# A fused embedding, attention and expert kernel: a hardware loop written out, first loads on two semaphores, one fill in place of two, and a broadcast that reads SBUF instead of DRAM

## What is computed

```
h   = concat(x @ W_tok + pe,  text embedding of x_txt)            # (16, 1101, 128)
y   = layernorm(h)
q, k, v = y @ wq, y @ wk, y @ wv                                   # per head, 64 wide
o   = softmax(q @ k.T / 8) @ v
h   = h + concat_heads(o) @ head_kernel
f   = layernorm(h) * ln_scale + ln_bias
out = h + swiglu(f @ shared_in.T) @ shared_out.T + b
        + sum over the 2 best of 4 experts of the better group: weight_e * (swiglu(f @ expert_in.T) @ W_e.T + b_e)
```

## Time and profile before

| | us |
|---|---|
| three runs | 4684.33, 4683.44, 4683.88 |
| median | 4683.88 |
| the profiled execution's own time | 4684.45 |
| its span, first to last instruction | 4682.7 |
| TensorE busy | 4476.3 |
| VectorE, ScalarE, GpSimd busy | 3215.6, 2298.7, 2943.6 |

### The profile page before, as it was taken

The page is one execution under the profiler, slowest core; times in us unless marked ns, Lnnn a source line. Parts: engine busy times, 40 slices in busy tenths (PEclk is TensorE's granted clock), DMA queues, the critical chain, the costliest instruction groups (busy, mean ns, idle before and its releaser), DMA issues.

```text
span 4682.7 us, 93178 instructions
## 1 busy us (share of the span) xinstructions
PE 4476.3 (96%) x26597; PEld 3324.5 (71%) x26597; DVE 3215.6 (69%) x7726; ACT 2298.7 (49%) x5640; POOL 2943.6 (63%) x1803
## 2 busy tenths in 40 slices
PE   5999999999999999999999999999999999999996
PEld 3667767777677776767777677776767777677765
DVE  5557767677675776768677675776767677686754
ACT  1555545445544555545545444555445455455441
POOL 0776666666666666666666666666666666666661
PEclk7999999999999999999999999999999999999998
DMA  2111111111101111111111111111011111111000
GB/s 53 35 34 41 33 30 40 39 25 34 45 24 39 32 32 40 30 33 40 33 32 34 32 37 39 25 34 45 25 38 35 30 39 34 30 40 37 21 21 19
DMA packets 157061, 159.01 MB, mean 34 GB/s; under 512 B 66576, under 2 KB 148359, under 8 KB 156551
## 3 DMA queue, kind: packets, MB, share of 16 engines
q1 hardware_dynamic: 156551, 152.68, 13.4%
HBM read 59.63 MB, written 19.65 MB: 17 GB/s over the span
## 4 chain that ended last, share of the span: by engine, by line
PE 84%; issue 4%; DVE 4%; DMA 3%; ACT 3%; POOL 1%; DVEq 0%; ACTq 0%; SPq 0%; POOLq 0%
PE o_ps L791 23%; PE work L688 12%; PE scores L772 12%; PE scores L774 11%; PE work L747 9%; PE work L680 4%; PE work L731 3%; PE work L673 2%; DMA sums<-inverse_rows 2%; PE work L708 2%; PE work L699 2%; PE work L736 1%; ACT probs L877 1%; DVE part_max L935 1%; POOL sums L1165 1%
## 5 line engine op out<-in xcount | busy, mean ns | idle before, releaser
L1165 POOL TENSOR_TENSOR sums<-sums,probs 128x736 f32<-128x736 f32 (+3 forms) x1344 | 2363.4, 1758 | 838.7 <-ACT probs L877 780.8
L877 ACT ACTIVATE probs<-scores 128x368 f32<-128x368 f32 (+3 forms) x3456 | 1460.2, 475 | 1542.5 <-PE scores L774 1487.1
L935 DVE TENSOR_REDUCE part_max<-work 128x1 f32<-128x368 f32 (+3 forms) x3456 | 1655.3, 530 | 449.5 <-PE work L688 439.1
L772 PE MATMUL scores<-q_a,k_a 128*128 128x368 f32 (+3 forms) x3456 | 1191.7, 345 | 84.0 <-issue 43.3
L791 PE MATMUL o_ps<-probs,values 128*64 128x368 f32 (+1 forms) x6912 | 1219.2, 489 | 1.6 <-ACT probs L877 0.2
L774 PE MATMUL scores<-q_b,k_b 128*128 128x368 f32 (+3 forms) x3456 | 1147.5, 332 | 0.0
L688 PE MATMUL work<-k_a,q_a 128*128 128x368 f32 (+3 forms) x3456 | 928.8, 352 | 9.1 <-DMA q_a<-q_b 8.1
L791 PEld LDWEIGHTS o_ps<-probs,values 128*64 128x64 f32 (+1 forms) x6912 | 453.0, 138 | 539.0 <-issue 447.1
L772 PEld LDWEIGHTS scores<-q_a,k_a 128*128 128x128 f32 (+1 forms) x3456 | 636.3, 184 | 200.4 <-ACT probs L877 77.9
L688 PEld LDWEIGHTS work<-k_a,q_a 128*128 128x128 f32 (+1 forms) x3456 | 595.0, 185 | 234.2 <-issue 208.8
L774 PEld LDWEIGHTS scores<-q_b,k_b 128*128 128x128 f32 (+1 forms) x3456 | 639.9, 185 | 17.4 <-issue 4.2
(11 more groups left out here) (183 smaller groups left out, 4493.1 us busy)
## 6 DMA issues: line engine op xcount, KB each, us to landing
sums<-inverse_rows SPq DMA_DIRECT2D x192, 184.0 KB
k_a<-k_a SPq DMA_DIRECT2D x128, 184.0 KB, 2.7
q_a<-q_b SPq DMA_DIRECT2D x128, 184.0 KB, 2.7
k_a<-k_a SPq DMA_DIRECT2D x64, 183.0 KB, 2.7
q_a<-q_b SPq DMA_DIRECT2D x64, 183.0 KB, 2.7
resid_rows<-heads_t SPq DMA_DIRECT2D x16, 576.0 KB, 6.2
h_out<-resid_rows SPq DMA_DIRECT2D x16, 576.0 KB, 8.0
heads_t<-in_pe_table_dram SPq DMA_DIRECT2D x16, 512.0 KB
```

What stands on the lines that cost most here:

```text
L772: nc.tensor.matmul(o, k_a[p % 2][i][:, t * P:t * P + n], q_a[p % 2][i][:, c0:c0 + cw], start=True, stop=False)
L877: nc.scalar.activation(probs[0:n, slot(s), i, 0:cw], scores[0:n, h % SB, 0:cw], ACT.Exp, scale=DH ** -0.5).then_inc(probs_ready, 1)
L935: nc.vector.tensor_reduce(part_max[0:n, i * IMG + j if j < IMG else 2 * IMG + i, c:c + 1], w[0:n, 0:keys], AX.X, ALU.max).then_inc(drained ...
L1165: nc.gpsimd.tensor_tensor(acc, acc, probs[0:n, slot(s), :, 0:cw], ALU.add).then_inc(sums_done, 1)
```

## The change

Four edits are made together.

1. The middle batches are written out: `for b in range(1, B - 1)` in place of the hardware loop. All counts become constants.
2. The first loads are split over two semaphores. The six small ones (position, nesting and segment tables, text weights, gates) go on `small_loaded`; the 22 others stay on `raw_loaded`. TensorE's first wait is for the six; it waits for the 22 ahead of the weight transposes. The load of `wo` (256 KB) moves to the end of the loads.
3. Rows 64 to 127 of each `k_b` tile are filled with ones in one instruction. Rows 65 to 127 meet zeros of `q_b`, so products are unchanged.
4. The inverses are stored to `sums[0:2, q % 2, 1, :]`, two rows of SBUF, instead of DRAM, and spread from there.

```diff
+    small_loaded = sem("small_loaded")
...
-            sp.dma_start(pos_raw[:], pos[0:TXT, :]).then_inc(raw_loaded, 16)
+            sp.dma_start(pos_raw[:], pos[0:TXT, :]).then_inc(small_loaded, 16)
...
-            sp.dma_start(wo[:], head_w.rearrange("(a p) n -> p a n", p=P)).then_inc(raw_loaded, 16)
...
+            sp.dma_start(wo[:], head_w.rearrange("(a p) n -> p a n", p=P)).then_inc(raw_loaded, 16)
             sp.wait_ge(s_taken, 11)
...
-            pe.wait_ge(raw_loaded, 16 * 28)
+            pe.wait_ge(small_loaded, 16 * 6)
             pe.wait_ge(s_pool, 2)
...
+            pe.wait_ge(raw_loaded, 16 * 22)
             for g, group in enumerate(groups):
...
-        with eng.Fori(1, B - 1) as b:
+        for b in range(1, B - 1):
             iteration(loop, b - 1, b)
...
-                then(nc.vector.memset(k_b[r][i][64:128, :].bitcast(F32), 0.0))
-                nc.vector.memset(k_b[r][i][64:65, :].bitcast(F32), 1.0)
+                nc.vector.memset(k_b[r][i][64:128, :].bitcast(F32), 1.0)
...
-            sp.dma_start(inv_dram[q % 2].rearrange("(a n) -> a n", n=RW), inv_cols[:]).then_inc(cols_stored, 16)
+            two_rows = sums[0:2, q % 2, 1, :]
+            sp.dma_start(two_rows.rearrange("p (a n) -> p a n", n=RW), inv_cols[:]).then_inc(cols_stored, 16)
...
-            two_rows = inv_dram[q % 2].rearrange("(i n) -> i n", i=2)
+            two_rows = sums[0:2, q % 2, 1, :]
             sp.dma_start(sums[:, q % 2, 0, :], two_rows.unsqueeze(1).broadcast_to((2, DH, CHUNK))).then_inc(
                 inverse_loaded[q % 2], 16)
```

More of the change, by code:

```diff
@@ L229, in fusion_kernel @@
     text_dram = nc.dram_tensor("text_rows", (B, TXT, D), F32, kind="Internal").ap()
-    inv_dram = nc.dram_tensor("inverse_rows", (2, 2 * CHUNK), F32, kind="Internal").ap()
     resid_dram = nc.dram_tensor("resid_rows", (B, P, NT * D), F32, kind="Internal").ap()
@@ L318, in _ @@
             sp.dma_start(tok_i[:], x_txt).then_inc(loaded, 16)
-            sp.dma_start(pos_raw[:], pos[0:TXT, :]).then_inc(raw_loaded, 16)
[L320 to L324, removed]
+            sp.dma_start(pos_raw[:], pos[0:TXT, :]).then_inc(small_loaded, 16)
+            sp.dma_start(tab_raw[0:NEST, :], nest).then_inc(small_loaded, 16)
+            sp.dma_start(tab_raw[NEST:NEST + SEG, :], seg).then_inc(small_loaded, 16)
+            sp.dma_start(txt_wr[:], txt_w.rearrange("(a p) n -> p a n", p=P)).then_inc(small_loaded, 16)
+            sp.dma_start(gates_raw[0:2, :], group_w).then_inc(small_loaded, 16)
+            sp.dma_start(gates_raw[2:2 + E, :], expert_w).then_inc(small_loaded, 16)
             sp.dma_start(in_raw[:, 0], sh_in.rearrange("(a p) n -> p a n", p=P)).then_inc(raw_loaded, 16)
@@ L344, in _ @@
             sp.wait_ge(s_stored, 16)
-            sp.wait_ge(raw_loaded, 16 * 28)
+            sp.wait_ge(raw_loaded, 16 * 22)
         in_turns = [(in_raw[:, w, a, :], P) for w in range(2) for a in range(4)]
@@ L390, in _ @@
         def _(act):
-            act.wait_ge(raw_loaded, 16 * 28)
+            act.wait_ge(raw_loaded, 16 * 22)
             v = attn_raw[:].rearrange("p (h w) n -> p w h n", w=3)
```

## The result

The changed kernel takes 4842.17 us (median of four, 4837.42 to 4842.66) against 4683.66 us. The ratio is 1.0336, 95% interval [1.0318, 1.0354]: slower by 158 us, where the prediction said 59, in a range that ended at 4795. The profiled execution has a span of 4840.0 us; the one of before had 4682.7, so the traces differ by 157.3 us and can be set against each other.

A forecast was written before the change was run, and what follows sets the result against it. TensorE, busy 96% of the span, plus its waits was taken as the bound. From 4684.45 us, -11.8 - 5.5 - 22.5 + 34.5 + 1.7 + 34.5 + 25.5 + 2.3 = +58.7 gave 4743 us, range 4630 to 4795.

The forecast's parts named there:

- The start: Before the first scores: small loads on their own semaphore, -11.8 us, and one fill for two, -5.5 us.
- The loop inside a batch: Inside a middle batch, straight code was to cost TensorE the same as the loop: 0 us.
- The sign of being wrong that I had named: Straight middle batches taking over 97.3 us from one L699 to the fifth after it, a fetching cost put at nothing.
- The loop at the boundaries: Last score tile to L699 in the next batch: 15.85 us instead of 17.58 at 13 boundaries, -22.5 us.
- The other end of my range: The 13 boundaries at 12.80 us each, as measured from batch 0 to batch 1: -62 us.
- The price of the spread: Each spread of inverses from SBUF takes 1.9 us more, with bounds from 4 us less to 3.6 us more.
- the store: Storing the inverses to SBUF takes 0.4 us more than the 1.56 us to DRAM, or up to 0.4 less.
- Step 9: TensorE waits at L708 for heads GpSimd scales: +34.5 us over 15 batches, and 25.5 us of lost clock.
- Step 3: The query copy queues behind a spread and the load: +34.5 us over 15 batches, 1.7 us of clock in batch 1.
- The other ten items: Their spreads are waited for by GpSimd, with over a third of its time free: 0, at most 1 us a batch.
- The rivals: Spread no dearer, 4605 to 4645 us (0.20); slower but hidden, 4678 us (0.07); spread goes wide, 4592 us (0.06).

The follow-up runs named there:

- the kernel with DRAM inverses: The changed kernel with one edit undone, so that the inverses are stored to DRAM and spread from there again: 4621.46 us, ratio 0.9865.
- the two kernels with spreads of 5.8 and 5.3 us: The changed kernel spreading only the first half of the columns, 4608.83 us; and the changed kernel with the two rows in partitions 0 and 64, 4603.99 us.

## Why the prediction was wrong

**Direction and mechanism held.** Slower, because the spread from two neighbouring partitions is slower than from DRAM, with TensorE behind it in steps 3 and 9: all of that was seen. The size was not: 158 us in place of 59, outside the range.

**The start**, -17.3: the traces have -17.0. With two semaphores the fills of `k_b` begin at 33.47 instead of 45.25 us (-11.8, as predicted); with one fill each, they and what follows end 5.1 us sooner (5.5 predicted). The issue that waits behind the large loads is now that of `ln_cols`, with 6.30 us, and nobody waits for it.

**The loop inside a batch**, "0": 1.4 us a middle batch, 18 to 19 us in all. The rows were there and I rounded their difference away. The sign of being wrong that I had named, more than 97.3 us between those L699, came with 101.0 us in batch 8, but it doesn't speak for fetching: with the loop alone written out it is 97.3 us, and most of the other 3.7 comes from steps 23 to 32.

**The loop at the boundaries**, 15.85 us for each: the step that failed first. Two straight boundaries were to be had, and I chose the one at the end for its traffic. Without the new spread the middle ones take 12.62. In batch 15, and in batch 15 alone, the load of `h_out` lands after 9.5 us in the kernel with DRAM inverses as well, against 8.0 in the middle; why, is open. The other end of my range, -62, was nearer: -67 measured.

**The price of the spread**, +1.9, and of the store, +0.4: +2.4 and +0.5, both inside their bounds. In the sum of 31 places 0.7 us more would have been 22 us. Partitions 0 and 1 as one feed was named and priced at 6.9 us of data; it is one feed, and the data take 7.7 us. The store took 1.93 us to SBUF and 1.41 to DRAM. The Trainium skill, "DMA: Bandwidth & Descriptors", section "Anatomy of one DMA — SWDGE (gpsimd) path", has the write to HBM as the dearer, for DMAs issued from GpSimd. These are issued from SyncE, and here the one to DRAM is the cheaper; but by the trace's semaphore records it has four shares and the one to SBUF two, so no run compares the two targets alone.

**Step 9**, 60 us: 66 to 67 measured, 4.47 us a batch, which is the 3.0 of store and spread and 1.5 of clock. This step was right, clock included, with store and spread 0.7 us dearer than taken and the clock 0.2 us cheaper.

**Step 3**, 36 us on top of a boundary that was 3.2 us too long to begin with: 65.5 measured against the DRAM kernel. A boundary of 18.15 us was forecast and 16.91 came, so the two errors cancel in part, and it is luck that the number comes near. The forecast had the wait and the half clock in it, since batch 15 showed both; what it had wrong is that the middle boundaries would have them without the new spread too. They get them from it: without it TensorE waits at most 0.6 us in the middle ones, and with it 2.8 to 3.6. The 4.0 us behind it, up to step 9, were forecast as 0.

**The other ten items**, "0, at most 1 us a batch": this is the step that made the result. I asked only who waits for the spread itself, and the answer was GpSimd, with time to spare. I didn't ask what is queued behind it on its two DMA engines. At one item, in step 30, the first key and query copies of a new pair of heads stand there, and cost 58 us over the batches, with clock. GpSimd's spare time didn't hold everywhere either. In batch 7 it ends one stretch of work at 2158.3, waits for the spread until 2159.66 and then has a run of additions to catch up on, until 2172.69 without a pause. In that run three of VectorE's operations take 1.8 to 2.0 us each; the one of L1029 that writes `e_tmp` takes 1.79 us here and 0.20 in the kernel with DRAM inverses, where GpSimd is idle at that moment. ScalarE waits for VectorE's result before it gets to its exponentials, and TensorE stands still for those in step 25:

```profile
2159.66 0.99 POOL L1136 TENSOR_TENSOR heads_t<-sums,heads_t 128x368 f32<-128x368 f32 x1 [1.37 <-DMA sums<-sums]
```

```profile
2169.05 1.79 DVE e_tmp L1029
2170.98 1.77 DVE e_sel L1032
```

```profile
2175.18 0.39 PE L773 MATMUL scores<-q_a,k_a 128*77 128x366 f32 x1 [0.87 <-ACT probs L878]
```

The middle two rows are from the chain of waits that leads to step 25. ScalarE's wait for `e_sel` (L1040) is 3.44 us on average over 15 batches, and 2.36 with DRAM inverses. The difference of 1.08 us is what step 25 loses in a batch; step 23 loses another 0.33. These are the 1.4 us of steps 14 to 30, 21 us in all. The same slow operations delay the inversion of the next item: with DRAM inverses it ends 9.4 us before TensorE's step 28, in the changed kernel 6.7 us before. So the spread that holds up step 30 lands 5.5 us later against TensorE than with DRAM inverses, and only 2.8 us of that are the length of the spread itself and of its store. A late spread makes the next one start later. That GpSimd's additions are what slows VectorE is read from their overlap; in the two kernels with spreads of 5.8 and 5.3 us the inversion is back at 9.3 and 9.4 us before step 28, but no run tests the two engines apart. GpSimd's waits for the spread went from 377.4 to 839.9 us, 2.4 us for each of 192 items: an engine that is free for a third of the time on average isn't free at each place.

**The sum.** With the sizes of the traces it is -16.2 for the start, -45.8 for the loop (boundaries -66.7, inside +18.7, and 2.2 at the end) and +219.4 for the inverses: +157.4, against 157.3 in the spans. Each term comes from the traces of the changed kernel, of the one with DRAM inverses and of the one before.

**The rivals.** None of them came true. What I took for the favourable case, -62 at the boundaries, held in the middle of an unfavourable one, and could only be seen where the spread was short.

## What to carry to other kernels

When a transfer gets longer, look at what is issued behind it on the same DMA engines, not only at who waits for it: a copy over sixteen engines is late when two of them are. Look also at where in SBUF a transfer reads that repeats a few rows; with the rows in partitions of different feeds this kernel's change is worth -80 us, and with neighbouring ones +158. And treat a stall that is taken away as a cover that is taken away: the branch of the loop had hidden the late copies at 13 boundaries.

## What the runs showed that I had not expected

- The feed of a partition can be read off a flat line in the rates: 24 to 29 GB/s for rows in partitions 0 and 1, the same landing for 0 and 32 (9.2 us), 47 to 53 GB/s for 0 and 64.
- From neighbouring rows of SBUF sixteen DMA engines are hardly faster than two: 8.5 us for a pair of wide copies, 9.25 for the narrow one. From DRAM they are: 3.3 us against 6.8.
- A late spread delays the next one: GpSimd catches up without a pause, three operations of VectorE beside it take 1.8 to 2.0 us, and the next inversion ends 2.7 us later against TensorE's steps.
- The time bends sharply with the length of the spread: 4604 us at 5.3 us, 4609 at 5.8, 4621 at 6.8, 4842 at 9.25 (the 5.8 us with half the data).
- Straight code costs TensorE 1.4 us in the 98 last steps of a middle batch against the same code in a loop, without a wait that the profile names.
- A store of 2.9 KB from columns takes 1.93 us to partitions 0 and 1 and 1.80 to 0 and 64, in two shares, and 1.41 to DRAM, in four.
